# Layer 0's queries by Strassen products in four slots, and the output projection ahead of them in three

## The reference, cut to what matters

```python
x = _rmsnorm(hidden_states, ln_weight)                  # hidden_states = layernorm of x
h_q = (x @ w_q.T).reshape(b, lq, 32, 128)               # 1024 tokens, 512 -> 32 heads x 128
h_k = (key_value_states @ w_k.T).reshape(b, lk, 32, 128)
h_v = (key_value_states @ w_v.T).reshape(b, lk, 32, 128)
score = jnp.einsum('bqhd,bkhd->bhqk', h_q, h_k) + position_bias[None]
score = softmax over the keys that the mask leaves
attn = jnp.einsum('bhqk,bkhd->bqhd', score, h_v).reshape(b, lq, 32 * 128)
out = attn @ w_out.T                                     # 4096 -> 512
x = x + tanh(g_xattn[0]) * (hidden_states + out)
```

## Time and profile before

| | |
|---|---|
| Median of 3 runs | 1748.13 us (1747.45 to 1748.26) |
| Profiled execution | 1748.51 us, its span 1746.3 us |
| TensorE, matmuls | 1695.1 us busy, 97% |
| TensorE, weight loads (beside the matmuls) | 1529.8 us, 88% |
| VectorE | 1188.1 us, 68% |
| ScalarE | 892.4 us, 51% |
| POOL | 557.3 us, 32% |
| Chain that ended last | TensorE 90% of the span |

### The profile page before, as it was taken

How to read it: one execution, slowest core, us unless ns; L and a number is a source line. 1 busy time by engine, 2 the same in 40 slices (tenths; PEclk the granted TensorE clock), 3 DMA queues, 4 the chain that set the end, 5 groups by cost and what they waited for, 6 DMA issues and landing times.

```text
span 1746.3 us, 31656 instructions
## 1 busy us (share of the span) xinstructions
PE 1695.1 (97%) x10935; PEld 1529.8 (88%) x10935; DVE 1188.1 (68%) x2247; ACT 892.4 (51%) x2370; POOL 557.3 (32%) x535
## 2 busy tenths in 40 slices
PE   7999999999899999999997899999999999999998
PEld 6999999988899999999996688888888888888887
DVE  6444437556777777777767876767777777777676
ACT  4344344335454544545443266666666666666663
POOL 4222223201522222222223433333333333333343
PEclk9999999999999999999999999999999999999999
DMA  6444344444333333323322010111111111111001
GB/s 233 154 157 156 144 171 153 170 138 156 107 109 96 109 109 105 108 94 108 111 67 99 8 58 29 49 37 48 36 45 36 39 45 36 48 36 35 17 7 48
DMA packets 80590, 153.31 MB, mean 88 GB/s; under 512 B 6544, under 2 KB 58128, under 8 KB 76944
## 3 DMA queue, kind: packets, MB, share of 16 engines
q1 hardware_dynamic: 80528, 152.50, 25.9%
HBM read 108.43 MB, written 44.04 MB: 87 GB/s over the span
## 4 chain that ended last, share of the span: by engine, by line
PE 90%; DVE 5%; DMA 2%; ACT 1%; issue 1%; POOL 1%; SPq 0%; DVEq 0%; ACTq 0%; POOLq 0%
PE bank L1768 20%; PE bank L1720 18%; PE bank L1722 18%; PE bank L1721 18%; PE bank L1926 3%; PE bank L2076 3%; PE bank L1883 3%; PE bank L1871 2%; PE bank L2102 2%; PE bank L1974 1%; DMA vraw<-wv 1%; PE bank L2107 1%; DMA plain<-w 1%; PE bank L1737 1%; DVE vw_lo L1124 0%
## 5 line engine op out<-in xcount | busy, mean ns | idle before, releaser
L1720 PE MATMUL bank<-w_hi,xt_hi 128*128 (+2 forms) x512 | 178.5, 349 | 2.7 <-issue 1.2
L626 POOL TENSOR_TENSOR pr<-pr,rn 128x512 f32<-128x512 f32 x64 | 66.7, 1043 | 347.4 <-DVE rn L1354 347.4
L1722 PE MATMUL bank<-w_hi,xt_lo 128*128 (+2 forms) x512 | 173.4, 339 | 0.0
L685 POOL TENSOR_TENSOR p<-p,rn 128x512 f32<-128x512 f32 x128 | 133.3, 1042 | 121.9 <-DVE rn L1598 118.6
L1721 PE MATMUL bank<-w_lo,xt_hi 128*128 (+2 forms) x512 | 172.0, 336 | 0.0
L1720 PE MATMUL bank<-xt_hi,w0q_hi 128*128 128x256 f32 x512 | 149.8, 293 | 0.0
L1721 PE MATMUL bank<-xt_lo,w0q_hi 128*128 128x256 f32 x512 | 144.5, 282 | 0.0
L1006 ACT ACTIVATE p<-bank,nb,q_r 128x256 f32<-128x256 f32 x256 | 141.2, 562 | 6.3 <-DVE nb L1593 3.9
L1722 PE MATMUL bank<-xt_hi,w0q_lo 128*128 128x256 f32 x512 | 144.4, 282 | 0.0
L908 ACT ACTIVATE ptr<-bank 128x512 f32<-128x512 f32 x63 | 37.7, 598 | 188.1 <-PE bank L1871 188.1
L552 POOL TENSOR_TENSOR q_r<-q_ms,half 128x4 f32<-128x4 f32 x64 | 64.5, 1008 | 192.2 <-DVE q_ms L1573 192.2
(11 more groups left out here) (227 smaller groups left out, 5487.4 us busy)
## 6 DMA issues: line engine op xcount, KB each, us to landing
stage<-w SPq DMA_DIRECT2D x35, 512.0 KB, 3.2
keys_of_layer<-kout SPq DMA_DIRECT2D x16, 1024.0 KB, 4.3
values_of_layer<-vout SPq DMA_DIRECT2D x16, 1024.0 KB, 4.8
kt<-keys_of_layer SPq DMA_DIRECT2D x64, 256.0 KB, 3.0
vs<-values_of_layer SPq DMA_DIRECT2D x64, 256.0 KB, 2.8
vraw<-wv SPq DMA_DIRECT2D x12, 1024.0 KB, 6.8
kraw<-wk SPq DMA_DIRECT2D x16, 512.0 KB, 5.2
stage0q<-w SPq DMA_DIRECT2D x16, 512.0 KB, 4.0
```

Of the source, the lines that this page charges most:

```text
L626: pool.tensor_tensor(by4(pr), by4(pr), rn[:, :].unsqueeze(2).to_broadcast([P, 4, P]), ALU.mult).then_inc(norm_done, 1)
L685: pool.tensor_tensor(p1[:, half_p:half_p + 2, :], p1[:, half_p:half_p + 2, :], rn1[:, half_p:half_p + 2].unsqueeze(2).to_broadcast([P, 2, ...
L1720: nc.tensor.matmul(out_ap, l_hi, r_hi, start=(c == 0), stop=False)
L1722: op = nc.tensor.matmul(out_ap, l_lo, r_hi, start=False, stop=(c == n - 1))
```

## The change

Groups 0 and 1 keep the old queries, but all eight units of them are made before slot 4 (`first_queries`: one ahead of the loop, then one, two, two and two in slots 0 to 3). For groups 2 to 15 the queries are made a group ahead, by seven Strassen products of six 512-column matmuls each (products 1 and 2 in the slot p = 0, 6 and 7 in p = 1, 5 in p = 2, 3 and 4 in p = 3), so 42 matmuls where the old way has 96. The queries of a whole group stand in `queries_of_layer_0`. The weight's sums are formed by POOL in p = 2, its high parts by ScalarE in p = 1 and p = 3, its low parts by VectorE in p = 1 and the following p = 0; the differences T1 to T4 of x are formed once, in slots 0 to 3, and split in slots 1 to 5. VectorE makes no dequantise step in p = 0 and two in p = 3. TensorE's output projection moves from the end of the slot to right behind the transposes, except in p = 3, in the first eight slots and in the last four. `accumulate` and `output_projection` themselves are not changed.

```diff
@@ SP, slot
-                if p in (1, 3) and not last:
-                    w = p // 2
-                    sp.wait_ge(w_lo_done[w], n + 2)
-                    load_weight(w, n + 2)
+                if p == 1 and not last and not (isinstance(t, int) and t == 0 and j == 1):
+                    load_query_weight(n + 2)
+                if p == 3 and not last:
+                    sp.wait_ge(w_lo_done[1], n + 2)
+                    load_weight(1, n + 2)
@@ POOL, slot
+                if j % 4 == 2 and not last:
+                    m = query_weight(2 * t + j // 4 + 2)
+                    weight_sums(qraw, kraw_in, ksum_done, m, m - 1)
@@ ScalarE
+            def query_part(n, par, p):
+
+                if p == 0:
+                    act.wait_ge(product_done, of_queries(1, n))
+                    act.wait_ge(s_ps, 4 * (n - 1))
+                    nc.scalar.activation(queries_of[:, par, 0, 0:512], bank[0][:, :], ACT.Copy).then_inc(part1_done, 1)
+                if p == 1:
+                    act.wait_ge(product_done, of_queries(6, n))
...
+                if p == 3:
+                    act.wait_ge(product_done, of_queries(3, n))
+                    nc.scalar.activation(queries_of[:, par, 0, 512:1024], bank[0][:, :], ACT.Copy).then_inc(c12_done, 1)
@@ ScalarE, slot
                 exponentials(i + 1)
-                if not (first and j == 0) and not (last and j == BODY - 1):
-                    queries_out(i + 2)
+                if first and 1 <= j < 4:
+                    queries_out(2 * j + 1)
+                    queries_out(2 * j + 2)
+                if not (first and j < 4) and not (last and j >= 4):
+                    query_part(n + 1, 1 - parity, p)
                 if not (first and j == 0):
                     output_hi(i, j - 1)
...
+                if first and 1 <= j < 5:
+                    query_difference_hi(j - 1)
+                if p == 1 and not last:
+                    query_weight_early(n + 2)
+                if p == 2 and not (last and j >= 4):
+                    act.wait_ge(w_in[1], 16 * (n + 2))
+                    wait(act, y_ps, 4 * n)
+                    nc.scalar.activation(w0_hi[1][1 - parity][:, :], stage0[1][:, :], ACT.Copy).then_inc(w_hi_done[1], 1)
+                if p == 3 and not last:
+                    query_weight_late(n + 2)
@@ VectorE
+            def quarter22_of_queries(n, par):
+                dve.wait_ge(product_done, of_queries(7, n))
+                dve.wait_ge(part4_done, query_job(n))
+                place = queries_of[:, par, 1, 512:1024]
+                nc.vector.tensor_tensor(place, place, bank[2][:, :], ALU.add).then_inc(c22_done, 1)
@@ VectorE, slot (maxima and accumulate stand above, unchanged)
+                if active and p == 0:
+                    query_weight_late_lo(n + 1)
+                if active and p == 3:
+                    quarter21_of_queries(n + 1, 1 - parity)
                 inverse_sums(i + 1, 2 * (j % 4))
                 if lag1:
                     output_lo(i, (j - 1) % 2)
-                if p in (0, 2) and not (last and j >= 4):
-                    w = p // 2
-                    dve.wait_ge(w_hi_done[w], n + 2)
-                    nc.vector.tensor_tensor(w0_lo[w][1 - parity][:, :], stage0[w][:, :],
-                                            w0_hi[w][1 - parity][:, :].bitcast(fp32), ALU.subtract).then_inc(w_lo_done[w], 1)
-                dequantise(2 * t + j // 4, j % 4, i + 1)
...
+                if first and j < 4:
+                    query_difference(j)
+                if first and 4 <= j < 6:
+                    query_difference_lo((T2, T1)[j - 4], (9, 11)[j - 4])
+                    query_difference_lo((T3, T4)[j - 4], (10, 12)[j - 4])
+                if active and p == 0:
+                    quarter11_of_queries(n + 1, 1 - parity)
+                if active and p == 2:
+                    quarter22_of_queries(n + 1, 1 - parity)
+                if p == 1 and not last:
+                    query_weight_early_lo(n + 2)
+                if p == 2 and not (last and j >= 4):
+                    dve.wait_ge(w_hi_done[1], n + 2)
+                    nc.vector.tensor_tensor(w0_lo[1][1 - parity][:, :], stage0[1][:, :],
+                                            w0_hi[1][1 - parity][:, :].bitcast(fp32), ALU.subtract).then_inc(w_lo_done[1], 1)
+                if p in (1, 2):
+                    dequantise(n, p - 1, i)
+                if p == 3:
+                    dequantise(n, 2, i)
+                    dequantise(n, 3, i + 1)
@@ TensorE
+            def query_product(number, which, start):
+                a, x_hi, x_lo = QUERY_BLOCKS[number]
+                for c in range(2):
+                    for l, r in ((qw_hi, x_hi), (qw_hi, x_lo), (qw_lo, x_hi)):
+                        op = nc.tensor.matmul(bank[which][:, :], l[:, a, c, :], r[:, c, :], start=start, stop=False, skip_group_check=True)
+                        start = False
+                op.then_inc(product_done, 1)
+
+            def query_products(n, p):
...
+                if p == 3:
+                    pe.wait_ge(part4_done, job)
+                    query_product(3, 0, False)
+                    if first:
+                        pe.wait_ge(t_lo_done, 12)
+                    pe.wait_ge(c22_done, job + 1)
+                    query_product(4, 2, False)
@@ TensorE, slot
                 if not (first and j == 0):
                     transposed_probabilities(i)
-                if not (last and j == BODY - 1):
-                    queries0(t + (j + 1) // BODY, (j + 1) % BODY)
+                late_output = p == 3 or first or (last and j >= 4)
+                if not late_output:
+                    output_projection(i - 1, (j - 2) % BODY, 2 * t + (j - 2) // 4)
+                if first and j < 4:
+                    for k in QUERIES_IN_SLOT[j]:
+                        first_queries(k)
+                elif not (last and j >= 4):
+                    query_products(n + 1, p)
                 if not (first and j == 0):
                     if not isinstance(t, int):
                         pe.wait_ge(v_in[(j - 1) % 2], 16 * (4 * t + (j + 1) // 2))
                     attention_output(i, (j - 1) % 2)
-                if not (first and j < 2):
+                if late_output and not (first and j < 2):
                     output_projection(i - 1, (j - 2) % BODY, 2 * t + (j - 2) // 4)
```

More of the change, by code:

```diff
@@ L78, in build @@
             kvc = place.enter_context(nc.sbuf_tensor("keys_values_of_context", [P, 2, 256], fp32))
+        with ExitStack() as place:
+            qt_t_hi = place.enter_context(nc.sbuf_tensor("qt_t_hi", [P, 4, 2, 512], fp32r))
+            with ExitStack() as same:
+                qt_t_raw = same.enter_context(nc.sbuf_tensor("qt_t_raw", [P, 4, 2, 512], fp32))
+            qt_t_lo = place.enter_context(nc.sbuf_tensor("qt_t_lo", [P, 4, 2, 512], fp32r))
         ct_hi = keep("ct_hi", [P, C, B * P], fp32r)
@@ L485, in _ @@
             sp.dma_start(fbias[:, :], ffn0_bias.to_broadcast([P, D])).then_inc(fbias_in, 16)
-            for piece, used, count in ((2, w_lo_done[1], NG), (0, q_ps, U - 4), (1, y_ps, U - 4), (3, added, U), (4, s_ps, U)):
+            for piece, used, count in ((2, w_lo_done[1], NG), (0, s_ps, U), (1, y_ps, U - 4), (3, added, U), (4, s_ps, U)):
                 sp.wait_ge(used, count)
@@ new lines, in quarter21_of_queries, with query_weight_early_lo @@
+            def quarter21_of_queries(n, par):
+                dve.wait_ge(product_done, of_queries(4, n))
+                dve.wait_ge(part2_done, query_job(n))
+                place = queries_of[:, par, 1, 0:512]
+                nc.vector.tensor_tensor(place, place, bank[2][:, :], ALU.add).then_inc(c21_done, 1)
+            def query_weight_early_lo(n):
+                low_part(qw_lo[:, EARLY, :, :], qraw[:, EARLY, :, :], qw_hi[:, EARLY, :, :], kw_hi_done, 2 * query_weight(n) + 1, kw_lo_done)
@@ new lines, in query_weight_late_lo, with query_difference @@
+            def query_weight_late_lo(n):
+                low_part(qw_lo[:, LATE, :, :], qraw[:, LATE, :, :], qw_hi[:, LATE, :, :], kw_hi_done, 2 * query_weight(n) + 2, kw_lo_done)
+            x_hi = lambda k, n: quarter(xt_hi, k, n).bitcast(fp32)
+            x_lo = lambda k, n: quarter(xt_lo, k, n).bitcast(fp32)
+            raw_t = lambda d: qt_t_raw[:, d, :, :]
+            def query_difference(d):
+                dst = raw_t(d)
+                if d in (T1, T3):
+                    one, other = ((0, 1), (0, 0)) if d == T1 else ((1, 1), (0, 1))
+                    link(nc.vector.tensor_tensor(dst, x_hi(*one), x_hi(*other), ALU.subtract))
+                    link(nc.vector.tensor_tensor(dst, dst, x_lo(*one), ALU.add))
+                    nc.vector.tensor_tensor(dst, dst, x_lo(*other), ALU.subtract).then_inc(diff_done, 1)
+                else:
+                    block_of, less = ((1, 1), T1) if d == T2 else ((1, 0), T2)
+                    dve.wait_ge(diff_done, 5 + less)
```

(12 more changed lines are left out.)

121 lines of the change are left out of this document (100 added, 21 removed).

## The result

The changed kernel takes 1999.78 us (median of four runs, 1997.22 to 2003.55) against 1747.91 (four runs): a ratio of 1.144, 95% interval 1.142 to 1.147. The profiled execution took 2002.32 us, with a span of 2000.4 (1746.3 before) and a mean granted clock of 0.948 (0.991 before).

A forecast was written before the change was run, and what follows sets the result against it. TensorE was taken to bound the kernel, never stopping in layer 0's attention loop. 1748.5 (profiled execution) + 161 (ring) + 9 (ends) + 68 (clock) = 1987 us; range 1900 to 2045.

The forecast's parts named there:

- a ring with a falling clock: Main case: in slots 8 to 59 waits close a ring and TensorE's clock falls; 1987 us, chance 0.73.
- the clock: Slots 8 to 59: holes before projections drop TensorE to 1.2 GHz, 3.5 stretches of 1.5 us a group; +68 us.
- the ring: Slots 8 to 59: accumulation, projection, products, attention output, ot_hi, ot_lo and next scores' sum wait in turn; +161 us.
- the ends: First eight and last four slots of the loop, and the loads of layer 1's weights: +9 us together.
- The wait: Early projection waits for VectorE's second accumulation, so it starts 2.88 us after that slot's sum of scores starts (T).
- a stretch of 1.5: One hole's assumed cost from TensorE running at 1.2 GHz afterwards: some 1.5 us.
- p=3: Last slot of each group, from T to next T: 7.21 us, with two dequantise steps, 2.36 us.
- this stretching: Dequantise steps lengthened beside POOL, 0.97 against 0.54: 22 us, only in the range's upper end.
- 78: Clock cost in us if, by the Trainium skill, all four holes of a group count, in place of 68.
- 8 + 3: Growth in us: slots 0 to 3 +8 (4 to 12), slots 4 to 7 +3 (-2 to +6).
- the tail: Last slot: VectorE dequantises twice and layer 1's weight loads wait for the last step; +1.2 us.
- What was said to cost nothing: ScalarE's copies and rounding, POOL's sums in p = 2, SP's query weight load, product 4's wait: nothing.

The follow-up runs named there:

- experiments 2 to 4: Projection moved early on the kernel before: 2009.27 us; on the changed kernel, experiment 3: 1940.40; or p = 1, 2 dequantise steps ahead of ot_lo: 1961.63.
- experiment 3: Changed kernel with useless 512-column matmuls in the holes ahead of the projections of slots 8 to 59: 1940.40 us, ratio 1.110.
- Experiments 9 and 10: Experiment 7's kernel with first difference instructions in VectorE's gaps, fourth low part in slot 6: 1746.91 us; experiment 10 on top: 1743.55 us.
- experiment 10: Kernel of 1746.91 us (VectorE's gaps in slots 0 to 7 filled), residual rows scaled by ScalarE instead of POOL: 1743.55 us, ratio 0.9970.
- Experiment 1: Changed kernel with the output projection at the end of every slot, products kept: 1772.86 us, ratio 1.014.
- experiment 7: Experiment 1's kernel with one dequantise step in every slot, that of p = 1 ahead of ot_lo: 1752.89 us, ratio 1.0022.
- experiment 8: Changed kernel with POOL scaling only 8 of 512 columns of each residual row block: 2000.55 us.

## Why the prediction was right, step by step

The measured time is 12.8 us above the forecast and inside the range. Its main theory, a ring with a falling clock, is what experiments 2 to 4 show: the move alone makes the loss (2009), the filler takes the clock's part away (1940), and a step moved out of the ring shortens the slots by its own length (1962). That the number is this near is in part luck: the ring was 12 us too short, the clock 9 too dear, and the ends 12 too short.

**The wait** was placed at T+2.88 and stands there: the projection at 766.59 follows the sum of scores at 763.71 by 2.88 us.

**The ring**, from T to T, against the forecast. The clock can be taken out of the comparison with experiment 3, where it is 1.00 (sums of scores at 741.00 to 785.51). Of the changed kernel two groups in turn stand here, slots 28 to 31 and 32 to 35:

```
slot   forecast  clock up (exp. 3)  with a stretch of 1.5   slots 28-31  slots 32-35
p=0    11.45     11.40              12.95                   12.83        13.85
p=1    12.63     12.61              14.13                   14.17        12.58
p=2    12.38     12.31              13.88                   13.88        15.12
p=3     7.21      8.19              (no stretch)             8.19         8.36
sum    43.67     44.51                                      49.07        49.91
```

With the clock up three slots are right to 0.07 us. The term that was too small is p = 3: its first dequantise step took 1.44 us beside POOL's bias, where I counted 0.54. I had this stretching in the range (22 us above), not in the sum. With it the ring is 44.57: 13 x 0.9 = 12 us more than forecast. The starts for slots 32 to 35, behind the 812.78 shown above:

```profile
826.63 0.68 DVE L1411 TENSOR_TENSOR sc<-bank,bm 128x512 f32<-128x512 f32 x1
...
839.21 0.68 DVE L1411 TENSOR_TENSOR sc<-bank,bm 128x512 f32<-128x512 f32 x1
...
854.33 0.68 DVE L1411 TENSOR_TENSOR sc<-bank,bm 128x512 f32<-128x512 f32 x1
...
862.69 0.69 DVE L1411 TENSOR_TENSOR sc<-bank,bm 128x512 f32<-128x512 f32 x1
```

**The clock** was forecast at 3.5 stretches a group, 68 us. It cost 59 (experiment 3 against the changed kernel), 4.5 a group, as much as three stretches of 1.5. But which holes bring a stretch was not as I had it, and the group shown first is only one of the kinds. In 38 of the 52 slots from 8 to 59 four or more 512-column matmuls behind the hole step by 0.43 us, losing 1.4 to 2.8 us; in 14 they keep 0.23. The length of the hole alone doesn't tell them apart. The one of 2.03 us ahead of p = 3's projection left the steps at 0.23 in six groups, as the 1.97 one in the earlier trace rows did, and in seven it did not. Here is the slot just before the group shown first, where the steps turn to 0.43 after four matmuls:

```profile
758.20 0.47 PE L1863 MATMUL bank<-w0o_hi,ot_hi 128*128 128x512 f32 x1 [2.03 <-DVE residual L1420]
758.51 0.39 PE L1864 MATMUL bank<-w0o_lo,ot_hi 128*128 128x512 f32 x1
...
761.20 0.63 PE L1863 MATMUL bank<-w0o_hi,ot_hi 128*128 128x512 f32 x1
761.62 0.63 PE L1864 MATMUL bank<-w0o_lo,ot_hi 128*128 128x512 f32 x1
```

And a hole of 3.48 us (p = 1, slot 33) left eleven steps at 0.235:

```profile
829.50 0.47 PE L1863 MATMUL bank<-w0o_hi,ot_hi 128*128 128x512 f32 x1 [3.48 <-DVE residual L1420]
...
832.08 0.39 PE L1865 MATMUL bank<-w0o_hi,ot_lo 128*128 128x512 f32 x1
```

So the count of 3.5 came near the right sum without telling right which holes count, and what does tell them apart is left open. The Trainium skill (TensorE: Matmul & The Clock Gate, HAM oscillation) says that a loop whose bursts are parted by waits is throttled in every turn. The trace agrees in kind, with 0.86 between 700 and 800 us and a fall in each of the 13 groups; the sum that I had worked out by it, 78, was too high, since 14 of the 52 holes did no harm.

The ring's error of 12 and the clock's of 9 nearly cancel, and slots 8 to 59 came out at +230.6 against 161 + 68.

**The ends** hold nearly the whole miss: slots 0 to 7 grew by 22.7 where I said 8 + 3. The direction was right, VectorE's differences and low parts hold the next scores back, but the sizes were taken from an instruction that ran alone. Ten differences at 1.14 are 11.4 us, and they lasted 16.2; four low parts are 4.6, and they lasted 7.5. Slots 0 to 3 came to +14.4, above my bound of 12, slots 4 to 7 to +8.3, above my bound of 6. Experiments 9 and 10 bear out that VectorE sets these slots: filled gaps took 7.3 us off them, and another 2.1 went with POOL's scaling, as much as the ten differences became shorter (15.3 to 13.2 us together). Of the 12.2 us by which experiment 10's first eight slots still exceed the kernel before, no run shows the split between more query matmuls in slots 0 to 3 and VectorE. Slots 60 to 62 gave 1.8 back (forecast 3 for 60 to 63), the tail took 1.3 (forecast 1.2).

**What was said to cost nothing** mostly did: no wait for the query weight, the quarters or POOL's sums is among the larger ones. I had not asked what the products are worth once the order is repaired. Experiment 1 shows that they bring nothing then either, since in p = 2 the projection still waits for VectorE, which is busy 84% and uneven over the four slots; with its steps placed anew (experiment 7) they are worth 1.0 us a group, of the 1.86 that TensorE saves. Of the 0.8 that is missing, 0.5 is in slot p = 2: with one product it would be 1.25 + 1.39 + 0.81 + 2.85 = 6.30, but it takes 6.81, and its projection stands at S+3.97, which is slot 63 again, the bare wait for the second accumulation. The other 0.3 is left open.

## What to carry to other kernels

Before work is moved earlier on an engine, look up which semaphore it waits for and where the instruction that raises it stands in its own in-order queue: a wait that is met 1.15 us early in one order starts a ring through three engines in the other, at 227 us here without one more matmul. When an operation is moved to the front, its releaser has to be moved with it, and the place where the old and the new order meet needs the room of both. Where a kernel keeps its TensorE full, spread VectorE's work evenly over the slots before counting matmuls saved.

## What the chip did that I had not expected

VectorE's instructions with two fp32 operands in SBUF and POOL's slow each other down. A 1024-column difference took 1.21 or 1.22 us with POOL idle and mostly 1.58 to 2.19 beside it; two of POOL's scalings took 1.51 to 1.53 us with VectorE idle or at instructions of four columns, and 3.46 to 4.54 beside the differences; ScalarE did the same two in 1.51, beside a VectorE that kept 1.21. The number of columns doesn't explain POOL's time: in experiment 8 a scaling of 8 columns beside VectorE took up to 2.37 us. And a granted clock that falls can be bought back with useless matmuls: 46 of them a group, 4.5 us of each 49.0 saved.
